# A vision-transformer layer with sliding-window attention: second query halves read 132 keys as a block of 128 and a corner of 4, and patch parts go two to a step

## The chip, the cores and the metric

The kernel runs on one core of one Trainium2 chip. The metric is the device time of one execution in microseconds (us); lower is better. The core has a matrix engine (PE, with its weight loads listed as PEld), a vector engine (DVE), a scalar engine (ACT), a general engine (POOL) and a queue engine for transfers (SP). They run their own instruction streams in order and wait for each other on semaphores.

## The reference, cut to what matters

64 images of 224 x 224 are cut into 196 patches each and projected to 192 features; a class token makes 197 tokens. Then comes one layer: attention by four experts of 12 heads (16 features a head) with a sliding window, a gated output, and a feed-forward step in which each token goes to one of four experts.

```python
mask = (i[:, None] - i[None, :] >= 0) & (i[:, None] - i[None, :] < 64)
for e in range(4):
    q, k, v = (x @ w[e].T split into 12 heads of 16 for w in (wq, wk, wv))
    attn = softmax(where(mask, q @ k.T / 4, -1e30))
    outs.append((attn @ v) @ wo[e].T)
fused = concatenate(outs)
h = h + silu(fused @ w_gate.T) * (fused @ w_up.T)
h = h + expert_ffn(layernorm(h))     # top expert of four, gelu, 192 -> 768 -> 192
```

A query sees itself and the 63 tokens before it. Queries 128 to 196 therefore need keys 65 to 196 (132 keys), and keys 65 to 68 are seen by queries 128 to 131 only.

## The kernel before

The work is in three parts. A set-up splits all weights into a high and a low f16 part (products of f32 accuracy are made of three f16 ones), writes the feed-forward weights to memory and projects the first two images. A loop of 32 turns (`STEPS`) handles two images a turn. After it 36 tiles of 384 sorted tokens go through the feed-forward step.

One turn of the loop first makes 20 projections (queries, keys, and `v` in 8 pieces; `proj`), then the attention, then the gated output. SP stacks queries and keys by transfers (`stack_queries`, `stack_keys`) and copies rows of `v` (L640). The 197 tokens of an image are two halves, `ROWS` = 128 and 69 queries. The attention is cut into 64 units: unit u is (group g of 6 heads, half, three of its heads `HU`, image) by `unit_of`, so that four units of first halves and four of second halves alternate. A first half meets 128 keys, a second half 138 keys from token 59 on (`KW0`, `KWN`). The second half's keys are turned as two blocks of 69, and `v` holds for each image a tile of tokens 0 to 127, one of tokens 128 to 196, and a copy of tokens 59 to 127 (index 1).

The attention is a pipeline written out by hand; in step s

- PE makes `scores(s)` (mask product L684, score products L689) into one of three banks, a part of the next images' patch projection (`patch_at`, `patch_part`, three matmuls at L258; 24 parts in all), then `turn_p(s - 2)` (f32 transposes, L703) into one of three more banks, then `times_v(s - 5)` (matmuls at L240, the helper `product`);
- DVE copies the finished products once in four steps (L898), takes the minima of the scores (they are negated; L905), subtracts the high part of the turned probabilities to have the low part (L911, unit s - 4), and once in four steps takes reciprocals (L920);
- ACT casts the turned probabilities to f16 (L815, unit s - 3) and makes the exponentials of unit s, one instruction a head (L824);
- POOL adds and scales products (L851, L857). Before the units it moves `h_next` into `h_in` (L864, L865), which `h_moved` tells.

`turn_p(u)` waits for `pt_lo` of unit u - 3, since it writes the same bank, and `scores(u)` for the exponentials of unit u - 3. Patch parts wait once for `embedded`, when DVE has read the first half out of bank 7 (L325). From step 41 on the finished outputs are turned (L738), then gated (L747).

Of the kernel before, what the change touches and what calls it, by code (L numbers as in the profile page):

```python
# [26 lines left out]
TOK = 197  # L27
# [6 lines left out]
E = 4  # L34
# [15 lines left out]
KW0 = (0, TOK - 2 * 69)  # L50
KWN = (128, 138)
# [39 lines left out]
def vit_layer(nc, x_t, wp, tok_bias, wqkv, wo, wgu, gate_w, gate_bc, w1, b1, w2, b2, ident, mask_id,  # L91
# [4 lines left out]
    with ExitStack() as ctx:  # L96
# [69 lines left out]
        pt = pt_f[:].rearrange("p (r s n) -> p r s n", r=PR, s=2)  # L166
        gated = pt_f[:, 0:8 * D].bitcast(F32).rearrange("p (t d) -> p t d", t=4)
# [307 lines left out]
        with nc.Block() as block:  # L475
# [20 lines left out]
            def _(dve):  # L496
# [14 lines left out]
                nc.vector.memset(early[:], FAR)  # L511

# [13 lines left out]
        def proj_psum(n):  # L526
            kind, j = proj[n]
            if kind == "v":
                return bank[n % PB][0:ROWS[j // 4], 0:2 * D]
            return bank[n % PB][:, 0:TP]  # L530

        def proj_target(n, part):
            kind, j = proj[n]
            if kind == "v":
                half, img, _, rows = tile_of(j // 2)
                return v[0:rows, img, 2 * half, 24 * (j % 2):24 * (j % 2) + 24, part * HD:part * HD + HD]
            return (kt if kind == "k" else qt)[:, j, part, :]
# [33 lines left out]

        def split_heads(ap):
            return ap.rearrange("p (h k) -> p h k", h=HU)
# [8 lines left out]
        PATCH_STEP, PATCH_GAP, PATCH_LAG = 0, 1, 1  # L582
# [11 lines left out]
        def patch_at(s):  # L594

            n, half = s - PATCH_STEP, 2 * PATCH_PARTS
            if 0 <= n < half:
                return n
            return n - PATCH_GAP if half <= n - PATCH_GAP < 2 * half else None
# [7 lines left out]
        with nc.Fori(0, STEPS, hint_back_edge=True) as i:  # L607
            with nc.Block(no_gpsimd_drain=True) as block:

                @block.sync  # L610
                def _(sp):
# [25 lines left out]
                    for img in range(PAIR):  # L637

                        sp.wait_ge(S["proj_lo"], v_first + 2 * img + 2)
                        sp.dma_start(v[0:69, img, 1], v[KW0[1]:128, img, 0]).then_inc(S["v_dup"], 16)  # L640
# [7 lines left out]
                def _(pe):  # L648

                    for n, (kind, j) in enumerate(proj):  # L650
# [9 lines left out]
                        if kind == "v":  # L660
                            _, _, c0, rows = tile_of(j // 2)
                            w0 = 2 * D * (j % 2)
                            passes = [(zt1[:, zi, c0:c0 + rows], wqkv_s[:, s, 2, blk, w0:w0 + 2 * D])
# [30 lines left out]
                    def turn_p(u):  # L694
                        _, half, _, _ = unit_of(u)
                        rows, kn, nk = ROWS[half], KWN[half], (128, 69)[half]
# [5 lines left out]
                        for b in range(HU * kn // nk):  # L702
                            mm = nc.tensor.transpose(bank[T_BANK + u % TR][0:nk, b * nk:b * nk + rows],  # L703
                                                     p_slot(u)[:, b * nk:b * nk + nk],
# [3 lines left out]
                    def times_v(u):  # L708
                        g, half, hh, img = unit_of(u)
                        w = u // 4  # L710
                        rows, nk = ROWS[half], (128, 69)[half]
# [7 lines left out]
                        for j in range(HU):  # L719
                            head = HG * g + HU * hh + j  # L720
                            passes = []
                            for b in range(1 + half):
                                c = ((1 + half) * j + b) * nk
                                passes += [(pt[0:nk, u % PR, s, c:c + rows], v[0:nk, img, half + b, head, :])
                                           for s in range(2)]
                            mm = product(o_bank(rows)[:, img, HU * hh + j, :], passes)
# [25 lines left out]
                    for s in range(PIPE):  # L752
                        if s < UNITS:
                            scores(s)
                        n = patch_at(s)
                        if n is not None:
# [37 lines left out]
                def _(act):  # L794
# [12 lines left out]
                    for s in range(PIPE):  # L807
                        u = s - LAG_HI
                        if 0 <= u < UNITS:
                            half = unit_of(u)[1]  # L810
                            nk, n = (128, 69)[half], HU * KWN[half]
# [3 lines left out]
                            nc.scalar.copy(pt[0:nk, u % PR, 0, 0:n], bank[T_BANK + u % TR][0:nk, 0:n]  # L815
# [56 lines left out]
                def _(dve):  # L872
# [18 lines left out]
                    for s in range(PIPE):  # L891
# [15 lines left out]
                        if 0 <= u < UNITS:  # L907
                            half = unit_of(u)[1]
                            nk, n = (128, 69)[half], HU * KWN[half]
                            dve.wait_ge(S["pt_hi"], u + 1)  # L910
                            nc.vector.tensor_tensor(pt[0:nk, u % PR, 1, 0:n], bank[T_BANK + u % TR][0:nk, 0:n],  # L911
                                                    pt[0:nk, u % PR, 0, 0:n], ALU.subtract
# [9 lines left out]
                        n = patch_at(s - PATCH_LAG)  # L922
                        if n is not None and (n + 1) % (2 * PATCH_PARTS) == 0:
# [372 lines left out]
```

## Time and profile before

| | us |
|---|---|
| median of 3 runs (4664.97 to 4667.81) | 4666.91 |
| the profiled execution | 4669.48 |
| its span, first to last instruction | 4667.7 |
| PE busy | 4077.5 (87%) |
| DVE busy | 3705.1 (79%) |
| ACT busy | 3196.0 (68%) |
| POOL busy | 1094.3 (23%) |

The span is what the profile shows from the first to the last instruction; the execution's time is 1.8 us longer. Times of one instruction are its duration, from issue to the end of its last write; matmuls overlap, so one that lasts 0.23 us can follow its forerunner by 0.06. A row of the timeline merges like instructions that follow each other: its first number is when the first begins, its second how long the merged stretch is, "x6" how many there are; in brackets stands how long the engine was idle before it and what ended that. `128*69 128x414` is a matmul with 128 rows of contraction and 69 weight columns, and 128 x 414 moving elements.

### The profile page before, as it was taken

The page shows a single profiled execution, that of the slowest core. Times are in us where ns is not written, and L with a number is a line of the kernel's source. Part 1 is how long each engine was busy: PE and PEld are TensorE (multiplying, and loading weights), DVE is VectorE, ACT ScalarE, POOL GpSimd, SP SyncE. Part 2 cuts the span into 40 slices and gives each one's busy share as a digit, 9 for nine tenths or more (in the row PEclk, how much of TensorE's full clock was granted, in tenths as well). Part 3 has the DMA queues.
Part 4 walks back from the last instruction along what each step waited for, and adds up shares of the span by engine and source line. Part 5 has one row for each costly group of instructions (what it writes and reads, how often), then busy time and mean ns, then how long its engine had stood idle before and what let it go on. Part 6 is the DMA issues. An engine that isn't in the chain of part 4 may idle for free. (4 is left out here: it accounts for less than half of the span.)

```text
span 4667.7 us, 129413 instructions
## 1 busy us (share of the span) xinstructions
PE 4077.5 (87%) x47470; PEld 3108.0 (67%) x47470; DVE 3705.1 (79%) x8870; ACT 3196.0 (68%) x9620; POOL 1094.3 (23%) x1496
## 2 busy tenths in 40 slices
PE   4889888888888998888888889888888888985998
PEld 2667666666666766666666667666666666764776
DVE  4888888888888888888888888888888888885665
ACT  2777777777777777777777777777777777772343
POOL 0222222222222222222222222222222222221222
PEclk7999999999999999999999999999999999997999
DMA  5122222111111222211111122222111111224664
GB/s 184 37 51 53 53 53 51 49 49 47 48 30 47 53 53 53 53 49 47 49 49 33 43 51 53 53 53 51 49 48 47 48 31 47 53 53 157 218 220 163
DMA packets 245909, 307.21 MB, mean 66 GB/s; under 512 B 56426, under 2 KB 223892, under 8 KB 235651
## 3 DMA queue, kind: packets, MB, share of 16 engines
q1 hardware_dynamic: 221794, 227.65, 18.7%
q10 hardware_dynamic: 4608, 38.73, 2.6%
q0 software_dynamic: 18912, 32.58, 2.0%
q8 instruction: 412, 6.75, 0.6%
q14 instruction: 183, 1.49, 0.1%
HBM read 127.06 MB, written 43.10 MB: 36 GB/s over the span
## 5 line engine op out<-in xcount | busy, mean ns | idle before, releaser
L824 ACT ACTIVATE p_s<-bank,smin 128x128 f32<-128x128 f32 (+1 forms) x6144 | 1894.6, 406 | 139.3 <-DVE smin L905 121.3
L905 DVE TENSOR_REDUCE smin<-bank 128x3 f32<-128x384 f32 (+1 forms) x2048 | 1157.4, 565 | 192.3 <-PE bank L689 134.0
L703 PE MATMUL bank<-ident_s,p_s 69*69 69x69 f32 (+1 forms) x9216 | 1093.5, 246 | 142.4 <-DVE pt_f L911 113.1
L911 DVE TENSOR_TENSOR pt_f<-bank,pt_f 128x384 f16<-128x384 f32 (+1 forms) x2048 | 1141.3, 560 | 28.5 <-ACT pt_f L815 28.5
L815 ACT CAST pt_f<-bank 128x384 f16<-128x384 f32 (+1 forms) x2048 | 1085.1, 532 | 52.1 <-PE bank L703 52.1
L703 PEld LDWEIGHTS bank<-ident_s,p_s 69*69 69x69 f32 (+1 forms) x9216 | 792.0, 141 | 363.9 <-issue 301.3
L240 PE MATMUL bank<-v_f,pt_f 69*69 69x33 f16 (+1 forms) x18432 | 881.8, 183 | 0.0
L240 PEld LDWEIGHTS bank<-v_f,pt_f 69*69 69x69 f16 (+1 forms) x18432 | 819.0, 110 | 36.9 <-issue 21.2
L684 PE MATMUL bank<-masks_s,mask_id_s 128*128 128x384 f16 (+1 forms) x2048 | 684.0, 334 | 38.9 <-DVE qt_f L876 24.4
L689 PE MATMUL bank<-stacks_f 128*128 128x256 f16 (+3 forms) x4096 | 686.3, 248 | 0.0
L851 POOL TENSOR_TENSOR w_s<-o_raw 128x192 f32<-128x192 f32 (+1 forms) x512 | 307.3, 600 | 1219.9 <-DVE o_raw L898 1219.9
L240 PE MATMUL bank<-zt,wqkv_s 128*128 128x394 f16 x1920 | 412.3, 379 | 170.4 <-PEq L961 164.0
L689 PEld LDWEIGHTS bank<-stacks_f 128*128 128x128 f16 (+1 forms) x4096 | 429.8, 105 | 131.2
L857 POOL TENSOR_TENSOR w_s<-w_s,o_rcp 128x192 f32<-128x192 f32 (+1 forms) x512 | 261.5, 511 | 780.7 <-DVE o_rcp L920 778.2
L240 PEld LDWEIGHTS bank<-zt,wqkv_s 128*128 128x128 f16 x1920 | 206.3, 110 | 357.5 <-issue 264.3
L747 PE MATMUL bank<-wgu_s,qt_f 128*128 128x384 f16 (+1 forms) x2304 | 405.8, 329 | 0.0
L258 PE MATMUL bank<-wp_s,x_s 128*69 128x192 f16 (+1 forms) x2376 | 324.2, 247 | 55.7 <-PEq L398 41.2
L898 DVE COPY o_raw<-bank 128x396 f32<-128x396 f32 (+1 forms) x512 | 287.3, 561 | 34.5 <-PE bank L240 34.5
L747 PEld LDWEIGHTS bank<-wgu_s,qt_f 128*128 128x128 f16 (+1 forms) x2304 | 235.6, 106 | 116.3 <-issue 4.2
L797 ACT ACTIVATE kt_f<-bank 128x394 f16<-128x394 f32 x192 | 95.9, 500 | 302.0 <-PE bank L240 302.0
L833 ACT CAST qt_f<-bank 128x394 f16<-128x394 f32 x192 | 95.8, 499 | 297.1 <-PE bank L738 297.1
L1155 ACT ACTIVATE gel<-bank,b_t 128x384 f32<-128x384 f32 x216 | 125.5, 581 | 229.4 <-PE bank L240 225.3
(116 smaller groups left out, 4449.7 us busy)
## 6 DMA issues: line engine op xcount, KB each, us to landing
stacks_f<-qt_f SPq DMA_DIRECT2D x768, 73.9 KB, 2.1
stacks_f<-kt_f SPq DMA_DIRECT2D x1536, 36.9 KB, 2.1
wx_t<-wx_d SPq DMA_DIRECT2D x36, 1344.0 KB
x_raw<-x_t_dram ACTq DMA_DIRECT2D x32, 1182.0 KB
rec_t<-rec_d SPq DMA_DIRECT2D x36, 678.0 KB, 4.1
v_f<-v_f SPq DMA_DIRECT2D x64, 213.5 KB
rec_d<-fill_s SPq DMA_DIRECT2D x5, 678.0 KB, 4.1
stacks_f<-w_dram SPq DMA_DIRECT2D x2, 1536.0 KB
```

The lines of the kernel that those rows point to most:

```text
L240: mm = nc.tensor.matmul(psum, stat, mov, start=(n == 0), stop=(n == len(passes) - 1))
L258: mm = nc.tensor.matmul(patch_psum(tt), *passes[p], start=(p == 0), stop=(p == len(passes) - 1))
L684: nc.tensor.matmul(ps, mask_id_s[:, 0:rows], masks_s[:, m0:m0 + HU * kn], start=True, stop=False)
L689: mm = nc.tensor.matmul(ps[:, j0 * kn:j1 * kn], qst[:, g % QS, two, q0:q0 + rows], kst[:, g % KS, h0 + j0:h0 + j1, k0:k0 + kn], start=Fals ...
L703: mm = nc.tensor.transpose(bank[T_BANK + u % TR][0:nk, b * nk:b * nk + rows], p_slot(u)[:, b * nk:b * nk + nk], ident_s[0:rows, 0:rows])
L747: mm = nc.tensor.matmul(bank[GU_BANKS[tt]][0:rows, 0:2 * D], ot[:, b, zi, c0:c0 + rows], wgu_s[:, s, b, :], start=(b == 0 and s == zi == 0 ...
L815: nc.scalar.copy(pt[0:nk, u % PR, 0, 0:n], bank[T_BANK + u % TR][0:nk, 0:n]).then_inc(S["pt_hi"], 1)
L824: ins = nc.scalar.activation(p_slot(s)[:, j * kn:j * kn + kn], bank[s % SR][0:rows, j * kn:j * kn + kn], ACT.Exp, scale=-1.0, bias=smin[0: ...
L851: nc.gpsimd.tensor_tensor(mine, o_raw[0:rows, w % 2, :, :, 0:HD], o_raw[0:rows, w % 2, :, :, HD:2 * HD], ALU.add).then_inc(S["o_summed"], 1)
L898: nc.vector.tensor_copy(o_raw[0:rows, w % 2], o_bank(rows)).then_inc(S["o_copied"], 1)
L905: nc.vector.tensor_reduce(least, ps, AX_X, ALU.min).then_inc(S["min_ready"], 1)
L911: nc.vector.tensor_tensor(pt[0:nk, u % PR, 1, 0:n], bank[T_BANK + u % TR][0:nk, 0:n], pt[0:nk, u % PR, 0, 0:n], ALU.subtract).then_inc(S[" ...
```

## The change

Second halves now take 132 keys, from token 65 on. Keys 69 to 196 are a block of 128 that is transposed as one. Keys 65 to 68, seen by the first four queries only, form the corner: an f32 matmul multiplies the probabilities of the first 128 of the 132 keys with the first four columns of the identity and so writes them, for four queries, into four columns beside the block. The turned unit is 3 x 73 = 219 columns over 128 rows, where it was 414 over 69. `times_v` then makes two pairs of products for each head as before, now over 128 rows: the block with a tile of `v` that holds tokens 69 to 196, and 69 columns of which four are the corner and 65 stay zero, with a tile of `v` whose first four rows are tokens 65 to 68 and whose others stay zero. These zeros are written once, in the set-up; the turned probabilities of second halves move to the room of `w1_s`, free once `wx_out` tells that the weights are written. The patch parts go two to a step, in steps 0 to 5 and 8 to 13, where they went one to a step, in 0 to 11 and 13 to 24.

```diff
--- before.py
+++ after.py
@@ -47,8 +47,11 @@
 HM = HID // 128
 ROWS = (128, TOK - 128)
 QW = (0, 128)
-KW0 = (0, TOK - 2 * 69)
-KWN = (128, 138)
+EDGE = 4
+KW0 = (0, TOK - 128 - EDGE)
+KWN = (128, 128 + EDGE)
+PTN = (128, TOK - 128 + EDGE)
+PT2 = 2 * (TOK - 128)
 UNITS = G * 8
 WSCALE = 256.0
 INV = 1.0 / WSCALE
@@ -164,6 +167,8 @@
         smin = sb1("smin", [128, XR, HU])
         pt_f = sb1("pt_f", [128, PR * 2 * HU * KWN[1]], F16)
         pt = pt_f[:].rearrange("p (r s n) -> p r s n", r=PR, s=2)
+        pt_late = w1_s[:].rearrange("p s b e n -> p (s b e n)")[:, 0:PR * 2 * HU * PT2].rearrange(
+            "p (r s n) -> p r s n", r=PR, s=2)
         gated = pt_f[:, 0:8 * D].bitcast(F32).rearrange("p (t d) -> p t d", t=4)
         o_raw = sb1("o_raw", [128, 2, PAIR, HG, VW])
         o_rcp = sb1("o_rcp", [128, 2, PAIR, HG, 1])
@@ -509,6 +514,9 @@
                 nc.vector.memset(zt2[:], 0.0)
                 nc.vector.memset(rec[:], 0.0)
                 nc.vector.memset(early[:], FAR)
+                nc.vector.memset(v[:, :, 1], 0.0)
+                dve.wait_ge(wx_out, 16 * (3 * E + 2))
+                nc.vector.memset(pt_late, 0.0)
 
         nc.all_engine_barrier(sems_to_clear=per_turn)
 
@@ -526,14 +534,14 @@
         def proj_psum(n):
             kind, j = proj[n]
             if kind == "v":
-                return bank[n % PB][0:ROWS[j // 4], 0:2 * D]
+                return bank[n % PB][:, 0:2 * D]
             return bank[n % PB][:, 0:TP]
 
         def proj_target(n, part):
             kind, j = proj[n]
             if kind == "v":
-                half, img, _, rows = tile_of(j // 2)
-                return v[0:rows, img, 2 * half, 24 * (j % 2):24 * (j % 2) + 24, part * HD:part * HD + HD]
+                half, img, _, _ = tile_of(j // 2)
+                return v[:, img, 2 * half, 24 * (j % 2):24 * (j % 2) + 24, part * HD:part * HD + HD]
             return (kt if kind == "k" else qt)[:, j, part, :]
 
         def proj_src(n):
@@ -569,6 +577,16 @@
             c0 = u % XR * HU * KWN[1]
             return p_s[0:ROWS[unit_of(u)[1]], c0:c0 + HU * KWN[unit_of(u)[1]]]
 
+        def probs(u, hl):
+
+            if unit_of(u)[1]:
+                return pt_late[:, u % PR, hl].rearrange("p (h n) -> p h n", h=HU)
+            return pt[:, u % PR, hl, 0:HU * 128].rearrange("p (h n) -> p h n", h=HU)
+
+        def turned_probs(u):
+            n = PTN[unit_of(u)[1]]
+            return bank[T_BANK + u % TR][:, 0:HU * n].rearrange("p (h n) -> p h n", h=HU)
+
         def split_heads(ap):
             return ap.rearrange("p (h k) -> p h k", h=HU)
 
@@ -579,7 +597,7 @@
 
         OT_STEP, OT_GAP, OT_HI, OT_LO = 41, 3, 1, 2
 
-        PATCH_STEP, PATCH_GAP, PATCH_LAG = 0, 1, 1
+        PATCH_STEP, PATCH_GAP, PATCH_LAG, PATCH_RATE = 0, 2, 1, 2
 
         GU_STEPS = {64: 0, 69: 1, 70: 2, 74: 3}
         LN_STEPS = (70, 74)
@@ -593,10 +611,12 @@
 
         def patch_at(s):
 
-            n, half = s - PATCH_STEP, 2 * PATCH_PARTS
+            half = 2 * PATCH_PARTS
+            n = PATCH_RATE * (s - PATCH_STEP)
             if 0 <= n < half:
-                return n
-            return n - PATCH_GAP if half <= n - PATCH_GAP < 2 * half else None
+                return range(n, n + PATCH_RATE)
+            n -= PATCH_RATE * PATCH_GAP
+            return range(n, n + PATCH_RATE) if half <= n < 2 * half else ()
 
         def turned_at(s):
 
@@ -637,7 +657,7 @@
                     for img in range(PAIR):
 
                         sp.wait_ge(S["proj_lo"], v_first + 2 * img + 2)
-                        sp.dma_start(v[0:69, img, 1], v[KW0[1]:128, img, 0]).then_inc(S["v_dup"], 16)
+                        sp.dma_start(v[0:EDGE, img, 1], v[KW0[1]:KW0[1] + EDGE, img, 0]).then_inc(S["v_dup"], 16)
                     stack_keys(1)
                     for g in range(1, G):
                         stack_queries(g)
@@ -658,9 +678,10 @@
                         if n >= PB:
                             pe.wait_ge(S["proj_lo"], n - PB + 1)
                         if kind == "v":
-                            _, _, c0, rows = tile_of(j // 2)
+                            _, _, c0, _ = tile_of(j // 2)
+                            c0 += j // 4 * (TOK - 256)
                             w0 = 2 * D * (j % 2)
-                            passes = [(zt1[:, zi, c0:c0 + rows], wqkv_s[:, s, 2, blk, w0:w0 + 2 * D])
+                            passes = [(zt1[:, zi, c0:c0 + 128], wqkv_s[:, s, 2, blk, w0:w0 + 2 * D])
                                       for s, blk, zi in D_PASSES]
                         else:
                             m = 0 if kind == "q" else 1
@@ -693,22 +714,28 @@
 
                     def turn_p(u):
                         _, half, _, _ = unit_of(u)
-                        rows, kn, nk = ROWS[half], KWN[half], (128, 69)[half]
+                        rows, kn = ROWS[half], KWN[half]
+                        turned = bank[T_BANK + u % TR]
                         pe.wait_ge(S["p_ready"], u + 1)
                         if u >= TR:
                             pe.wait_ge(S["pt_lo"], u - TR + 1)
                         else:
                             pe.wait_ge(S["proj_lo"], last_use(T_BANK + u))
-                        for b in range(HU * kn // nk):
-                            mm = nc.tensor.transpose(bank[T_BANK + u % TR][0:nk, b * nk:b * nk + rows],
-                                                     p_slot(u)[:, b * nk:b * nk + nk],
+                        for j in range(HU):
+                            c0, k0 = j * PTN[half], j * kn
+                            if half:
+                                nc.tensor.matmul(turned[:, c0 + rows:c0 + rows + EDGE],
+                                                 p_slot(u)[:, k0:k0 + 128], ident_s[0:rows, 0:EDGE],
+                                                 start=True, stop=True)
+                                k0 += EDGE
+                            mm = nc.tensor.transpose(turned[:, c0:c0 + rows], p_slot(u)[:, k0:k0 + 128],
                                                      ident_s[0:rows, 0:rows])
                         mm.then_inc(S["pt_mm"], 1)
 
                     def times_v(u):
                         g, half, hh, img = unit_of(u)
                         w = u // 4
-                        rows, nk = ROWS[half], (128, 69)[half]
+                        rows = ROWS[half]
                         pe.wait_ge(S["pt_lo"], u + 1)
                         if u == 0:
                             pe.wait_ge(S["lg_read"], 1)
@@ -718,12 +745,10 @@
                             pe.wait_ge(S["o_copied"], w)
                         for j in range(HU):
                             head = HG * g + HU * hh + j
-                            passes = []
-                            for b in range(1 + half):
-                                c = ((1 + half) * j + b) * nk
-                                passes += [(pt[0:nk, u % PR, s, c:c + rows], v[0:nk, img, half + b, head, :])
-                                           for s in range(2)]
-                            mm = product(o_bank(rows)[:, img, HU * hh + j, :], passes)
+                            o = o_bank(rows)[:, img, HU * hh + j, :]
+                            passes = [(probs(u, hl)[:, j, rows * b:rows * b + rows], v[:, img, 2 * half - b, head, :])
+                                      for b in range(1 + half) for hl in range(2)]
+                            mm = product(o, passes)
                         mm.then_inc(S["pv_mm"], 1)
 
                     def turn_o(e, blk):
@@ -752,8 +777,7 @@
                     for s in range(PIPE):
                         if s < UNITS:
                             scores(s)
-                        n = patch_at(s)
-                        if n is not None:
+                        for n in patch_at(s):
                             if n == 0:
                                 pe.wait_ge(S["x_lo"], 1)
                                 pe.wait_ge(S["pos_read"], 1)
@@ -808,11 +832,10 @@
                         u = s - LAG_HI
                         if 0 <= u < UNITS:
                             half = unit_of(u)[1]
-                            nk, n = (128, 69)[half], HU * KWN[half]
                             act.wait_ge(S["pt_mm"], u + 1)
                             if u >= PR:
                                 act.wait_ge(S["pv_mm"], u - PR + 1)
-                            nc.scalar.copy(pt[0:nk, u % PR, 0, 0:n], bank[T_BANK + u % TR][0:nk, 0:n]
+                            nc.scalar.copy(probs(u, 0)[:, :, 0:PTN[half]], turned_probs(u)
                                            ).then_inc(S["pt_hi"], 1)
                         if s < UNITS:
                             half = unit_of(s)[1]
@@ -906,10 +929,9 @@
                         u = s - LAG_LO
                         if 0 <= u < UNITS:
                             half = unit_of(u)[1]
-                            nk, n = (128, 69)[half], HU * KWN[half]
                             dve.wait_ge(S["pt_hi"], u + 1)
-                            nc.vector.tensor_tensor(pt[0:nk, u % PR, 1, 0:n], bank[T_BANK + u % TR][0:nk, 0:n],
-                                                    pt[0:nk, u % PR, 0, 0:n], ALU.subtract
+                            nc.vector.tensor_tensor(probs(u, 1)[:, :, 0:PTN[half]], turned_probs(u),
+                                                    probs(u, 0)[:, :, 0:PTN[half]], ALU.subtract
                                                     ).then_inc(S["pt_lo"], 1)
                         w = window_at(s, LAG_OR)
                         if w is not None:
@@ -919,8 +941,8 @@
                                 dve.wait_ge(S["o_ready"], w - 1)
                             nc.vector.reciprocal(o_rcp[0:rows, w % 2], o_raw[0:rows, w % 2, :, :, 2 * HD:VW]
                                                  ).then_inc(S["o_rcp_ready"], 1)
-                        n = patch_at(s - PATCH_LAG)
-                        if n is not None and (n + 1) % (2 * PATCH_PARTS) == 0:
+                        done = [n for n in patch_at(s - PATCH_LAG) if (n + 1) % (2 * PATCH_PARTS) == 0]
+                        for n in done:
                             half = n // (2 * PATCH_PARTS)
                             if half == 0:
                                 dve.wait_ge(S["h_moved"], 1)
```

## Rows read from the trace of the kernel before

**Rows 1.** The page: busy us of each engine, share of the span, instructions.

```profile
PE 4077.5 (87%) x47470; PEld 3108.0 (67%) x47470; DVE 3705.1 (79%) x8870; ACT 3196.0 (68%) x9620; POOL 1094.3 (23%) x1496
```

**Rows 2.** Table by stretches: length, busy us by engine (instructions), granted clock, DMA share, GB/s.

```profile
1016.81:1096.82 80.01, 75.01 (x1074) 62.38 (x1074) 73.92 (x164) 75.67 (x254) 19.89 (x32) 1.00 0.24 61
```

**Rows 3.** Timeline of PE in one turn: start us, length us, engine, line, operation, operands.

```profile
1016.81 0.32 PE L684 MATMUL bank<-masks_s,mask_id_s 128*128 128x384 f16 x1 [0.45 <-DVE kt_f L876]
...
1018.31 0.34 PE L684 MATMUL bank<-masks_s,mask_id_s 128*128 128x384 f16 x1 [0.76 <-DVE qt_f L876]
...
1018.65 0.41 PE L258 MATMUL bank<-wp_s,x_s 128*128 128x192 f16 x3
1018.90 0.33 PE L684 MATMUL bank<-masks_s,mask_id_s 128*128 128x384 f16 x1
...
1036.15 0.32 PE L684 MATMUL bank<-masks_s,mask_id_s 128*128 128x384 f16 x1
...
1051.24 0.56 PE L240 MATMUL bank<-v_f,pt_f 69*69 69x33 f16 x12
1051.65 0.34 PE L684 MATMUL bank<-masks_s,mask_id_s 128*69 128x414 f16 x1
...
1052.01 0.49 PE L703 MATMUL bank<-ident_s,p_s 128*128 128x128 f32 x3
1052.34 0.57 PE L240 MATMUL bank<-v_f,pt_f 69*69 69x33 f16 x12
...
1055.40 0.34 PE L684 MATMUL bank<-masks_s,mask_id_s 128*69 128x414 f16 x1
...
1056.36 0.32 PE L684 MATMUL bank<-masks_s,mask_id_s 128*128 128x384 f16 x1
...
1057.15 0.56 PE L703 MATMUL bank<-ident_s,p_s 69*69 69x69 f32 x6 [0.30 <-DVE pt_f L911]
1057.56 0.31 PE L240 MATMUL bank<-v_f,pt_f 128*128 128x33 f16 x6
1057.71 0.32 PE L684 MATMUL bank<-masks_s,mask_id_s 128*128 128x384 f16 x1
...
1066.23 0.32 PE L684 MATMUL bank<-masks_s,mask_id_s 128*128 128x384 f16 x1
...
1097.61 0.56 PE L703 MATMUL bank<-ident_s,p_s 69*69 69x69 f32 x6 [0.64 <-DVE pt_f L911]
```

**Rows 4.** Timeline of DVE in the same turn, steps 31 and 32.

```profile
1055.96 0.58 DVE L905 TENSOR_REDUCE smin<-bank 69x3 f32<-69x414 f32 x1 [0.16 <-PE bank L689]
1056.46 0.54 DVE L911 TENSOR_TENSOR pt_f<-bank,pt_f 128x384 f16<-128x384 f32 x1
```

**Rows 5.** Line L470, f32 products: durations min/median/max; whole run, its start, and timeline.

```profile
L470 PEld LDWEIGHTS bank<-kt_f,qt_f x32: 190/190/337, 14.6 to 27.0; 96*128 96x128 f32 x32
L470 PE MATMUL bank<-kt_f,qt_f x32: 486/486/1007, 14.6 to 27.3; 96*128 96x384 f32 x32
...
L470 PEld LDWEIGHTS bank<-kt_f,qt_f x2: 286/310/333, 14.6 to 14.8; 96*128 96x128 f32 x2
...
L470 PE MATMUL bank<-kt_f,qt_f x2: 847/927/1007, 14.6 to 15.4; 96*128 96x384 f32 x2
...
14.62 0.50 PEld L470 LDWEIGHTS bank<-kt_f,qt_f 96*128 96x128 f32 x2 [14.62 <-DMA kt_f<-wgu_dram]
```

**Rows 6.** Groups by line and shape: busy us, mean ns of one, idle us before them.

```profile
L911 DVE TENSOR_TENSOR pt_f<-bank,pt_f 69x414 f16<-69x414 f32 x1024 | 586.6, 575 | 28.5 <-ACT pt_f L815 28.5
L911 DVE TENSOR_TENSOR pt_f<-bank,pt_f 128x384 f16<-128x384 f32 x1024 | 557.3, 544 | 0.0
L703 PEld LDWEIGHTS bank<-ident_s,p_s 69*69 69x69 f32 x6144 | 467.3, 142 | 223.8 <-issue 189.1
```

**Rows 7.** Timeline of POOL in the same turn.

```profile
1008.89 0.50 POOL L865 COPY h_in<-h_next 69x384 f32<-69x384 f32 x1
```

**Rows 8.** The set-up: timeline of DVE, and table by stretches as in rows 2.

```profile
85.25 1.19 DVE L509 MEMSET zt<- 128x1359 f16 x1 [0.35 <-issue]
...
78.00:84.00 6.00, 2.59 (x16) 1.43 (x13) 4.11 (x15) 0.80 (x2) 0.77 (x1) 0.77 0.00 0
```

## The prediction

> **What bounds the kernel now.** I read the page first, then the loop's turns by stretches, then single steps. The page puts PE at 87% of the span, DVE at 79% and ACT at 68% [rows 1]: near each other, so it names no bound. The table by stretches shows that of one turn 80.0 us pass while its 64 units are scored, and in them PE, DVE and ACT all look over nine tenths full [rows 2]. With 32 turns this stage is 2560 us, over half the time. Busy times of matmuls overlap, so I read it from start to start.
>
> PE, at the upper clock level (granted clock 1.00 [rows 2]): scores of a first half take 0.34 us (1018.31 to 1018.65), of a second half 0.36 (1051.65 to 1052.01); a patch part 0.25 (1018.65 to 1018.90); `turn_p` of a first half 0.33 (1052.01 to 1052.34), of a second 0.41 (1057.15 to 1057.56), which falls to 0.39 where its first load is hidden; `times_v` 0.15 (1057.56 to 1057.71) and 0.41 (1051.24 to 1051.65) [rows 3]. Eight units come to 4 x 0.82 + 4 x 1.16 = 7.9 us. But step 32 begins at 1056.36 and step 40 at 1066.23: 9.87 us [rows 3]. PE alone is not the bound.
>
> What closes the step is a loop over two steps, and the rows show it whole. The scores of step 31 begin at 1055.40 [rows 3], the minima at 1055.96, the subtraction behind them at 1056.46, lasting 0.54 [rows 4]; only then may `turn_p` write its bank again, at 1057.15, "0.30 <-DVE"; `times_v` follows at 1057.56 and the scores of step 33 at 1057.71 [rows 3]. That is 2.31 us for two steps: 1.75 up to the turning, then 0.41 + 0.15. With the other combinations of halves (turning 0.33, `times_v` 0.41, a slower subtraction) the eight loops are about 2.31 three times, 2.6, 2.51 three times, 2.24, sum 19.3; each step lies in two, so eight steps take 9.65 us. DVE's two copies of `o_raw` ahead of minima add some 0.2. This meets the observed 9.87, so I price the change with this loop.
>
> **The change part by part.** *Corner products.* The six transposes of a second half (0.39 us, 0.06 each) become, for each of three heads, an f32 product with 128 weight columns and 4 moving ones, and a transpose with 128 weight columns and 69 moving ones, which I leave at 0.06. For the product the nearest rows are the 16 of L470. They are 32 records, two for each product, each with a weight load [rows 5]. With 384 moving columns the load is hidden there; with four it lies bare. Its price, first way: the first load starts at 14.62 and takes 0.286; the two loads together end 0.50 after 14.62, so 0.21 after the first. The matmul lasts 0.847 or more there and 0.486 later [rows 5], so this is the lower level, and at the upper one 0.21 is 0.105. Second way, at the upper level: a product's load lasts 0.190 [rows 5], a transposing load 0.142 [rows 6] with 0.06 from one to the next: 0.190 - 0.142 + 0.06 = 0.11. I take 0.11 a record: 3 x (2 x 0.11 + 0.06) = 0.84 us for the turning, +0.45 for each of the 32 second halves of a turn. From below I bound a record by a transposing load, 0.06 (turning 0.54); from above by 0.19, loads that overlap nothing (1.32). The value taken comes twice from rows of the same form, so it is far nearer than either end.
>
> A rule speaks against the change here. The Trainium skill, "TensorE: Matmul & The Clock Gate", section "LDWEIGHTS (loading the stationary operand)", says that a weight load costs its columns, whatever the depth of the contraction: P / 1.2 ns, 107 ns for 128 columns; few moving columns don't help. The Trainium skill, "FP8 and Floating Point Precision", section "TensorE Precision Notes", has four passes for true f32. The rows agree with the 107 ns and show two records, not four loads; by four, the turning would be an estimated 1.5 us, near my upper end.
>
> *Narrower second halves.* 396 score columns instead of 414 save 0.01 on PE and 0.02 in the minima. The subtraction runs over 219 columns instead of 414. Its two forms, 414 and 384 columns, last 0.575 and 0.544 [rows 6], 0.001 a column, so it gets 0.20 shorter; nothing, if the new strided operand eats it. ACT's cast shrinks in the same way, but ACT is not in the loop above. What pays is the 0.20 inside the loop, in four of eight steps.
>
> *`times_v` of second halves.* Twelve matmuls before and after, now over 128 rows of the contraction with 69 weight columns. The form is not shown; the two that are cost 0.41 / 12 = 0.034 and 0.15 / 6 = 0.025 a matmul [rows 3]. I leave 0.034; the other end would give back 0.1 a unit.
>
> *The new loop.* By turned unit (second halves first) the loops are 1.75 + 0.84 + 0.15 = 2.75 three times, 2.82, 2.30 three times, 2.23. PE's own work is 1.35, 1.35, 1.33, 1.58 in the steps that turn second halves and 1.07, 1.07, 1.09, 0.84 in the others, 9.7 us. Where the loop asks more than PE's own work the step is longer: 1.61, 1.35, 1.40, 1.58, 1.07, 1.23, 1.09, 1.14, and 0.15 for a copy, 10.6 us against 9.87, +0.75. Steps 16 to 63 are six such groups: +4.5 us.
>
> *Patch parts two a step.* The same 24 parts of 0.24, now in steps 0 to 5 and 8 to 13. Spread out they lay in gaps of the loop; step 9 will hold 0.33 + 0.48 + 0.84 + 0.41 = 2.06 us of PE alone, with `turn_p`, and so ACT's cast, queued behind the parts. Step 1 cannot start before 1018.31, 1.5 us after step 0 at 1016.81 [rows 3], since its bank waits for projections. From there PE needs 0.81, 1.14, 1.14, 1.16, 1.32, 1.35, 1.35 to step 8 and 1.81, 2.06, 1.55, 1.55, 1.57, 1.32, 1.35, 1.35 to step 16: 22.3 us with the 1.5. Before, step 16 began at 1036.15, after 19.3 [rows 3]: +3.0 us. The gap of two steps hides PE's wait for `embedded`. DVE's wait for `h_moved` moves up to step 6, with the minima queued behind it; POOL's second copy starts at 1008.89, long before [rows 7]: nothing.
>
> *Drain.* The turnings of units 62 and 63 come behind the last scores, the first at 1097.61 after waiting 0.64 for DVE [rows 3]: 2 x 0.45 less 0.2 of subtraction, +0.7.
>
> *Copies and projections of v.* The copy on SP's queue carries 4 rows instead of 69 and is due only in step 9; the second tiles' products get 128 weight columns instead of 69 under the same 384 moving ones: nothing.
>
> *Set-up.* DVE fills 3168 and 3312 more f16 at the end of a block. 1359 f16 took 1.19 us [rows 8], 0.88 ns each: 5.7 us, or half where two are filled as one word; +4 once. The new wait for `wx_out`, with these fills and the block's barrier behind it, costs nothing: the DMA share is already 0.00 from 78 to 84 us, before DVE gets there [rows 8].
>
> Sum: 3.0 + 4.5 + 0.7 = 8.2 us a turn; x 32 = 262; + 4 = 266. The profiled execution took 4669.5 us (span 4667.7): 4935.5. The median of the runs, 4666.9, lies 2.6 lower: **4933 us, 5.7% slower**. This case's own range: with no loop waits at all in steps 16 to 63 (+0 there) 32 x 3.7 + 4, 4790; with two microseconds more waiting a turn, 5000.
>
> **The rivals.** *Cheap products, faster* (the other side). If a four-column record costs what a transposing load costs, 0.06, the turning is 0.54 and the loops 2.45 three times, 2.5, 2.30 three times, 2.23: 19.0 against 19.3, and DVE has more room for its copies; some -0.4 us in eight steps, -2.4 over six groups, +0.7 in the crowded patch steps, +0.1 in the drain: -1.6 x 32 + 4, 4620 us. It decides below some 0.07 a record. For it: DVE and ACT do look full, and the change relieves both. Against: both ways of pricing the load.
>
> *Nothing moves.* At 0.07 to 0.08 a record gain and price meet, 4667.
>
> *Bare records.* At 0.19 a record PE alone needs 4 x 0.82 + 4 x 2.08 = 11.6 us in eight steps: +10.4 over six groups, +5.9 before step 16, +1.7 in the drain, 18 us a turn, 5240. For it: the switch between product and transpose is seen nowhere. Against: the first two loads of L470 follow each other without a gap [rows 5]. The four-pass rule, if it held in loads, would end near it.
>
> **How the numbers follow.** Forecast case 0.77, cheap products 0.12, nothing 0.04, bare records 0.07. A measurement here can tell about 0.2%, 9 us, from no change. Slower 0.84, same 0.04, faster 0.12. Leaving out the cheap case and most of the bare one, and leaning a little past the own range for record prices from 0.10 to 0.12, the range is 4730 to 5030.
>
> **What would show it.** Right: two records of an f32 product for each head, 0.11 apart; `turn_p` of a second half over 0.8 us; the subtraction of 219 columns 0.20 shorter and DVE idle before minima, waiting for PE; steps 32 to 40 in 10.6 us; step 9 over 2 us. Wrong: a turning under 0.55 us, or DVE still full.

## The result, and the profile after

The changed kernel takes 5491 us at the median of 4 runs (5486 to 5495), against 4667 for the kernel before on the same chip: ratio 1.1765, 95% interval 1.1745 to 1.1786. It is 17.6% slower; 5.7% was forecast, and the time lies 461 us above the range. The profiled execution has a span of 5488.4 us.

Here is the page after, with the same line as [rows 1] and the granted clock in 40 slices, in tenths (before, all but two of them were 9):

```profile
PE 4930.5 (90%) x50542; PEld 4004.3 (73%) x50542; DVE 3545.2 (65%) x8872; ACT 3133.8 (57%) x9620; POOL 1091.3 (20%) x1496
...
PEclk7888888888888888888888888888888888887999
```

DVE and ACT are relieved and stand at 65% and 57% of a longer span; PE has 3072 more matmuls. And the clock, which the forecast never asked about, is below nine tenths through the whole loop: mean 0.856 where it was 0.957.

The table by stretches of one turn shows where. The first line is steps 0 to 15 with all patch parts, the others follow up to step 43 (columns as in [rows 2]):

```profile
1198.76:1221.39 22.63, 22.11 (x289) 20.52 (x290) 16.87 (x42) 17.04 (x60) 6.64 (x8) 1.00 0.40 119
1221.39:1233.40 12.01, 11.60 (x162) 10.07 (x158) 9.50 (x23) 10.21 (x37) 2.22 (x4) 1.00 0.22 46
1233.40:1240.20 6.80, 6.80 (x61) 6.17 (x61) 3.23 (x9) 3.56 (x13) 1.11 (x2) 0.50 0.27 58
1240.20:1247.00 6.80, 6.40 (x88) 5.44 (x86) 5.29 (x13) 5.84 (x20) 1.10 (x2) 1.00 0.05 11
1247.00:1253.80 6.80, 6.80 (x59) 6.18 (x58) 3.13 (x9) 3.60 (x12) 1.11 (x2) 0.50 0.27 58
1253.80:1260.70 6.90, 6.50 (x89) 5.52 (x87) 5.47 (x13) 5.88 (x20) 1.11 (x2) 0.99 0.06 13
1260.70:1267.50 6.80, 6.80 (x59) 6.20 (x60) 2.82 (x8) 3.20 (x12) 0.91 (x2) 0.50 0.26 57
```

In this trace the clock holds the upper level while patch parts run (1.00), and 12 us more; from then on it changes between 0.50 and 1.00, and in the stretch shown it does so every 6.8 us. At 0.50 PE gets through 59 to 61 matmuls where it gets through 88 or 89 at 1.00, and it has no idle time in them. Summed from 110 us on, the lower level lasts 1518 us (337 before). On the mean of the 32 turns 33 us of it lie in the 101 us from the first scores to the last, all in steps 16 to 63; before there was none there, and its 337 us all lay outside (9.0 us a turn between the last scores and the next first ones). So the kernel before changed level too, but never within the stretch whose steps the forecast read.

The timeline of PE gives the price of the turning at each level. At the upper one (compare 1057.15 in [rows 3]):

```profile
1243.63 0.35 PE L727 MATMUL bank<-ident_s,p_s 69*128 69x4 f32 x2 [0.28 <-DVE pt_f L933]
1243.84 0.26 PE L731 MATMUL bank<-ident_s,p_s 69*128 69x69 f32 x1
1243.93 0.33 PE L727 MATMUL bank<-ident_s,p_s 69*128 69x4 f32 x2
...
1244.41 0.26 PE L731 MATMUL bank<-ident_s,p_s 69*128 69x69 f32 x1
1244.51 0.31 PE L245 MATMUL bank<-v_f,pt_f 128*128 128x33 f16 x6
1244.66 0.34 PE L705 MATMUL bank<-masks_s,mask_id_s 128*69 128x396 f16 x1
```

1243.63 to 1244.51 is 0.88 us, 0.29 a head, in two records for each product; 0.84 was forecast. At the lower level a like turning takes from 1248.28 to 1249.88, 1.60 us:

```profile
1248.28 0.53 PE L727 MATMUL bank<-ident_s,p_s 69*128 69x4 f32 x2
...
1249.88 0.89 PE L245 MATMUL bank<-v_f,w_s 128*69 128x33 f16 x12
```

Who waits for it is named in the waits of the kernel after (total us, times, longest); in the kernel before the first of these was 134.0, the second 121.3:

```profile
DVE smin L928 <- PE bank L710: 883.9, 1156, 2.8
ACT p_s L847 <- DVE smin L928: 863.1, 1414, 2.3
```

### The profile page after: what moved, and what is told of

Its sections match the earlier page's. It is cut to its first block and busy times, and to the rows that moved or that the text cites. A ratio compares the mean times of both kernels' runs of the same rounds, so it can differ in the third digit from the quotient of the medians.

```text
span 5488.4 us, 135559 instructions
## 1 busy us (share of the span) xinstructions
PE 4930.5 (90%) x50542; PEld 4004.3 (73%) x50542; DVE 3545.2 (65%) x8872; ACT 3133.8 (57%) x9620; POOL 1091.3 (20%) x1496
## 5 line engine op out<-in xcount | busy, mean ns | idle before, releaser
L731 PE MATMUL bank<-ident_s,p_s 128*128 128x128 f32 (+1 forms) x6144 | 1457.6, 295 | 16.1
L731 PEld LDWEIGHTS bank<-ident_s,p_s 128*128 128x128 f32 (+1 forms) x6144 | 1199.7, 209 | 60.3 <-issue 54.0
L727 PEld LDWEIGHTS bank<-ident_s,p_s 69*128 69x128 f32 x6144 | 1040.5, 229 | 145.6 <-issue 114.1
L727 PE MATMUL bank<-ident_s,p_s 69*128 69x4 f32 x6144 | 1051.2, 254 | 63.9 <-DVE pt_f L933 63.5
L245 PEld LDWEIGHTS bank<-v_f,w_s 128*69 128x69 f16 x12288 | 707.0, 137 | 7.3
L245 PE MATMUL bank<-v_f,w_s 128*69 128x33 f16 x12288 | 681.5, 199 | 0.0
L933 DVE TENSOR_TENSOR pt_f<-bank,pt_f 128x384 f16<-128x384 f32 x1024 | 556.8, 544 | 0.0
L838 ACT CAST pt_f<-bank 128x384 f16<-128x384 f32 x1024 | 496.4, 485 | 0.0
L838 ACT CAST w_s<-bank 128x219 f16<-128x219 f32 x1024 | 359.5, 351 | 152.5 <-PE bank L731 132.9
L933 DVE TENSOR_TENSOR w_s<-bank,w_s 128x219 f16<-128x219 f32 x1024 | 383.9, 378 | 88.8 <-ACT w_s L838 88.8
```

What stands on the lines that cost most here:

```text
L245: mm = nc.tensor.matmul(psum, stat, mov, start=(n == 0), stop=(n == len(passes) - 1))
L727: nc.tensor.matmul(turned[:, c0 + rows:c0 + rows + EDGE], p_slot(u)[:, k0:k0 + 128], ident_s[0:rows, 0:EDGE], start=True, stop=True)
L731: mm = nc.tensor.transpose(turned[:, c0:c0 + rows], p_slot(u)[:, k0:k0 + 128], ident_s[0:rows, 0:rows])
L838: nc.scalar.copy(probs(u, 0)[:, :, 0:PTN[half]], turned_probs(u)).then_inc(S["pt_hi"], 1)
L933: nc.vector.tensor_tensor(probs(u, 1)[:, :, 0:PTN[half]], turned_probs(u), probs(u, 0)[:, :, 0:PTN[half]], ALU.subtract).then_inc(S["pt_lo ...
```

## The experiments

Theory A: the corner products do it twice over. Their bare weight loads (loads that no moving columns cover) cost what the forecast said, and while they load, few columns move, and the clock falls. Theory B: the clock was held up by patch parts spread over 25 steps, and drawing them together let it fall. The runs came in three groups, each on a chip of its own, on which the kernel before took 4742, 4737 and 4710 us; so I compare ratios to the kernel before on the same chip: e1 to e4 are on the first of these, e5 to e8 on the second, e9 to e12 on the third. Clocks are those of each run's profiled execution.

| run | ratio, 95% interval | mean clock |
|---|---|---|
| the change | 1.1765 (1.1745 to 1.1786) | 0.856 |
| e1 before, two parts a step | 1.0074 (1.0047 to 1.0101) | 0.955 |
| e2 change, one part a step | 1.1761 (1.1698 to 1.1823) | 0.864 |
| e3 change, no corner | 0.9711 (0.9685 to 0.9737) | 0.957 |
| e4 change, 64 moving columns | 1.0948 (1.0916 to 1.0980) | 0.933 |
| e5 change, small transposes | 1.1650 (1.1594 to 1.1707) | 0.850 |
| e6 as e5, one part a step | 1.1563 (1.1538 to 1.1589) | 0.861 |
| e7 before, products added | 1.2355 (1.2316 to 1.2394) | 0.835 |
| e8 change, 32 moving columns | 1.1077 (1.1048 to 1.1107) | 0.920 |
| e9 change, full transposes | 0.9957 (0.9940 to 0.9973) | 0.958 |
| e10 as e9, one part a step | 0.9779 (0.9764 to 0.9793) | 0.967 |
| e11 the change again | 1.1866 (1.1823 to 1.1910) | 0.850 |
| e12 before again, one run | 4711.5 us | 0.966 |

**Which half of the change.** e1 gives the kernel before the new `patch_at`:

```diff
-        PATCH_STEP, PATCH_GAP, PATCH_LAG = 0, 1, 1
+        PATCH_STEP, PATCH_GAP, PATCH_LAG, PATCH_RATE = 0, 2, 1, 2
```

> The kernel before with the patch parts two to a step (steps 0 to 5 and 8 to 13) and nothing else of the change. Theory A (the corner products take the clock down: they keep PE occupied with weight loads while four columns move): the mean granted clock stays near 0.95 and only the crowded steps cost, 1 to 2 us a turn, so 4700 to 4730 us. Theory B (the patch parts spread over 25 steps had held the clock up, and drawing them into 14 steps lets it fall): the clock falls in steps 14 to 63, mean below 0.90, time 4900 us or more.

e2 takes it from the changed kernel:

```diff
-        PATCH_STEP, PATCH_GAP, PATCH_LAG, PATCH_RATE = 0, 2, 1, 2
+        PATCH_STEP, PATCH_GAP, PATCH_LAG, PATCH_RATE = 0, 1, 1, 1
```

> The changed kernel with its patch parts one to a step again (steps 0 to 11 and 13 to 24). Theory A: steps 0 to 24 hold the upper level as before, but steps 25 to 63 still fall, so 5300 to 5480 us, mean clock 0.86 to 0.89. Theory B: the clock is back near 0.95 and the time is that of the blind sum, 4900 to 4950 us.

The clock of e1 stays at 0.955 and that of e2 stays down at 0.864. Theory B falls as the cause of the loss. Patch parts do hold the clock where they run and shortly after: in steps 16 to 31 e2, with parts up to step 24, has no lower level at all and the change 11.0 us a turn, but from step 32 on e2 has 22.8 us (mean of 32 turns). Two parts a step cost 0.7% on the kernel before; e1 took 4778 us, more than the 4730 I gave, but on a chip where the kernel before takes 75 more. e2's 5565 lies above its 5480 for the same reason; its ratio is as that of the change.

**The corner.** e3 deletes the product, so keys 65 to 68 are left out for queries 128 to 131:

```diff
-                                nc.tensor.matmul(turned[:, c0 + rows:c0 + rows + EDGE],
-                                                 p_slot(u)[:, k0:k0 + 128], ident_s[0:rows, 0:EDGE],
-                                                 start=True, stop=True)
```

> The changed kernel without the three corner products of a second half; keys 65 to 68 are left out for queries 128 to 131. Theory A: clock back near 0.95, the turning of a second half about 0.2 us (three transposes), DVE and ACT relieved, so 4500 to 4620 us, below the kernel before. Theory B: the patch parts are still drawn together, so the clock still falls and the time is 4900 us or more. A third view, that the strided operands or the zero columns cost much, would show as more than 4750 us at a clock of 0.95.

Ratio 0.971 at a clock of 0.957, 4605 us, as Theory A wanted: three transposes in place of six, narrower scores, 219 columns and products over 128 rows together gain 2.9%, in spite of two parts a step. All of the loss is in the corner. e7 is the counterpart, the kernel before with nothing but the products:

```diff
+                        for j in range(HU * half):
+                            nc.tensor.matmul(bank[T_BANK + u % TR][:, 420 + 4 * j:424 + 4 * j],
+                                             p_slot(u)[:, j * kn:j * kn + 128], ident_s[0:rows, 0:4],
+                                             start=True, stop=True)
```

> The kernel before with the three f32 products of 128 weight columns and 4 moving columns added to each second half, their result going to unused columns of the bank; nothing else changed. Theory A: the products alone make both the price and the fall of the clock. At the upper level 0.6 us a second half, some 500 us in all; with the clock below 0.90 some 500 us more: 5500 to 5900 us, ratio 1.18 to 1.26. If the clock fell for another reason (operands over 128 rows, the narrower scores), it stays at 0.95 and the ratio is 1.09 to 1.13.

1.2355 and 0.835. Its PE timeline also has the six records alone, without transposes between them: 0.64 us, 0.107 a record, at the upper level.

```profile
1344.45 0.78 PE L703 MATMUL bank<-ident_s,p_s 69*128 69x4 f32 x6
1345.09 0.57 PE L707 MATMUL bank<-ident_s,p_s 69*69 69x69 f32 x6
```

**Load or clock.** e4 and e8 keep every instruction and every weight load, and only move more columns (e8 has 32 in both places):

```diff
-                                nc.tensor.matmul(turned[:, c0 + rows:c0 + rows + EDGE],
-                                                 p_slot(u)[:, k0:k0 + 128], ident_s[0:rows, 0:EDGE],
+                                nc.tensor.matmul(turned[:, c0 + rows:c0 + rows + 64],
+                                                 p_slot(u)[:, k0:k0 + 128], ident_s[0:rows, 0:64],
```

> The changed kernel with one size changed: each corner product moves 64 columns of the identity, not 4; the 60 extra ones are written over by the transposes behind. The same two records and the same weight loads, more work. Theory A, with the moving columns as what holds the clock: the clock rises to 0.93 or more and the time falls to 4900 to 5050 us although more is computed. If the clock looked at how long PE is occupied, or if the loads alone were the cost, the time stays at 5490 us or rises by up to 100 us.

> The changed kernel with 32 moving columns in each corner product, between the 4 of the change (ratio 1.177, clock 0.856) and the 64 of e4_wide_corner (1.095, 0.933). If the moving columns hold the clock, both lie between: ratio 1.12 to 1.16, clock 0.88 to 0.92. If 64 columns worked through another way (a longer matmul hiding a load), the clock stays at 0.856 and the ratio at 1.17 or above.

More work, less time: from 1.18 with 4 columns to 1.108 with 32 and 1.095 with 64, the clock going from 0.856 to 0.920 and 0.933. Their ends were a little off (e4 took 5185 us, not 5050 or less; e8's ratio is below 1.12). The turning of e4 costs at the upper level what that of the change costs, 0.29 us a head, so the columns bought nothing but clock.

Where they bought it shows in steps 16 to 63 of one turn, first of e4, then of the change (columns as in [rows 2]):

```profile
1160.21:1224.61 64.40, 62.08 (x865) 54.41 (x861) 52.05 (x122) 55.31 (x193) 12.79 (x23) 1.00 0.15 34
1221.39:1299.19 77.80, 75.46 (x865) 66.42 (x861) 52.36 (x122) 56.61 (x193) 12.78 (x23) 0.80 0.13 28
```

The same 865 matmuls, at 1.00 and at 0.80. In none of its 32 turns has e4 any lower level in these steps; e8 has 4.1 us a turn there, the change 32.8 (31.5 in e11, on another chip). What e4 has left of it, 8.2 us a turn, lies in steps 0 to 15. On its chip the kernel before with two parts a step (e1) has 2.5 us there too, and the change on the third chip (e11) 6.8, so that part depends on the chip as well.

Timeline of PE in e4, a head's records and the start of the next head's, and then the start of steps 32 and 40:

```profile
1206.03 0.38 PE L727 MATMUL bank<-ident_s,p_s 69*128 69x64 f32 x2
1206.25 0.23 PE L731 MATMUL bank<-ident_s,p_s 69*128 69x69 f32 x1
1206.32 0.38 PE L727 MATMUL bank<-ident_s,p_s 69*128 69x64 f32 x2
```

```profile
1181.88 0.32 PE L705 MATMUL bank<-masks_s,mask_id_s 128*128 128x384 f16 x1
...
1192.71 0.32 PE L705 MATMUL bank<-masks_s,mask_id_s 128*128 128x384 f16 x1
```

Between the last two lie 10.83 us, with the clock up. In the trace of the change itself, 29 of the 160 groups of eight steps between step 16 and 56 hold no lower level at all: they average 10.80 us, and steps 32 to 40 take 10.83 like those of e4. The 114 that hold more than 6 us of it average 14.46, with 7.9 us at the lower level. Of these 32 are steps 40 to 47, which with the clock up take 11.64 (e4); place by place the 114 would average 11.04 with the clock up. So (14.46 - 11.04) / 7.9 = 0.43 us are lost for each microsecond of the lower level.

**A smaller corner.** If bare loads of 128 columns cost so much, load four:

```diff
+                                nc.tensor.transpose(turned[0:EDGE, c0 + rows:c0 + rows + EDGE],
+                                                    p_slot(u)[0:EDGE, k0:k0 + EDGE], ident_s[0:EDGE, 0:EDGE])
```

> The changed kernel with the corner turned by a transpose of 4 rows and 4 columns (a weight load of 4 columns, 4 moving columns) in place of the f32 product with 128 weight columns; the rows 4 to 127 of those columns keep what the bank held and meet zero rows of v. Theory A: clock at 0.95 as without a corner, three more short matmuls of 0.03 to 0.06 us a second half, so a ratio of 0.97 to 0.985 to the kernel before. If a mode switch or an f32 matmul with few moving columns as such were at fault, the ratio stays above 1.05.

> As e5_small_corner, with the patch parts one to a step again. Drawing them together cost 0.7% on the kernel before, so this should be the fastest of all, ratio 0.955 to 0.975. If the two parts a step pay once DVE and ACT are relieved, it is slower than e5_small_corner.

Both were wrong by far: 1.165 and 1.156, clock 0.85 and 0.86, with no f32 product left. The timeline of e5 at the upper level says why the price stays:

```profile
1759.99 0.08 PEld L727 LDWEIGHTS bank<-ident_s,p_s 4*4 4x4 f32 x1
1759.99 0.16 PE L727 MATMUL bank<-ident_s,p_s 4*4 4x4 f32 x1
1760.08 0.14 PEld L730 LDWEIGHTS bank<-ident_s,p_s 69*128 69x128 f32 x1
1760.09 0.28 PE L730 MATMUL bank<-ident_s,p_s 69*128 69x69 f32 x1
...
1760.29 0.08 PEld L727 LDWEIGHTS bank<-ident_s,p_s 4*4 4x4 f32 x1
```

The small load begins 0.21 us after the full transpose in front of it started, where in e9 below one full transpose follows another after 0.06. A head takes 0.30 us, as with the product. So my wording of Theory A was too narrow: what the change, e5, e6 and e7 share is not the f32 product, but turnings of 0.9 us or more in which PE hardly moves columns, be it for bare loads or for small weights that wait. Why the small load starts so late is open.

**Full transposes.** e9 turns the corner's 128 keys for all 69 queries and lets the next head write over what is too much:

```diff
-                                nc.tensor.matmul(turned[:, c0 + rows:c0 + rows + EDGE],
-                                                 p_slot(u)[:, k0:k0 + 128], ident_s[0:rows, 0:EDGE],
-                                                 start=True, stop=True)
+                                nc.tensor.transpose(turned[:, c0 + rows:c0 + rows + rows],
+                                                    p_slot(u)[:, k0:k0 + 128], ident_s[0:rows, 0:rows])
```

> The changed kernel with each corner turned by a transpose of the same 128 keys for all 69 queries (128 weight columns, 69 moving ones) in place of the f32 product; the 65 columns too many are written over by the next head's, or lie behind the last. It has six transposes as the kernel before, 0.06 us apart, so a turning of 0.39 us, and no small weight tile. If the two losses are the bare loads and the clock, both go: clock 0.95 or more, ratio 0.975 to 0.995. If a corner as such costs (reading the probabilities twice, 128 weight columns), the ratio stays above 1.03.

> As e9_full_turn, with the patch parts one to a step again: 0.5 to 1% faster than e9_full_turn, ratio 0.965 to 0.99, below the kernel before. If two parts a step pay once DVE and ACT are relieved, it is slower than e9_full_turn.

Timeline of PE in e9; the turning lasts from 1205.53 to 1205.93, 0.40 us, as in [rows 3]:

```profile
1205.53 0.25 PE L727 MATMUL bank<-ident_s,p_s 69*128 69x69 f32 x1 [0.28 <-DVE pt_f L932]
1205.62 0.23 PE L730 MATMUL bank<-ident_s,p_s 69*128 69x69 f32 x1
1205.68 0.23 PE L727 MATMUL bank<-ident_s,p_s 69*128 69x69 f32 x1
...
1205.93 0.31 PE L245 MATMUL bank<-v_f,pt_f 128*128 128x33 f16 x6
```

Both losses are gone: 0.9957, just above the band, clock 0.958. With one part a step e10 takes 4605 us, ratio 0.978: 2.2% less than the kernel before, and 17.7% less than the change on the same chip (e11, 5593 us). Two parts a step cost 1.9% here (4692 against 4605), more than the 0.5 to 1% expected: steps 0 to 15 take 22.9 us in e9 and 20.7 in e10 (means of 32 turns).

**The same kernels on another chip.**

> The changed kernel itself, on the chip of the other experiments, for its ratio there: 1.17 to 1.18 as on the first chip, clock 0.86; so that e2_after_one_part, e4_wide_corner and e8_corner_32 are compared on one chip.

> The kernel before on this chip, for its profile: 4740 us where the first chip took 4667. If the 70 us are slower stacking transfers, the first eight steps of a turn wait on them and take more than the 7.9 us seen on the first chip, and steps 32 to 40 stay at 9.87.

The two ran on the chip of e9 and e10, not on those of e2, e4 and e8 as e11's expectation had it, and e12 took 4711 us, not 4740. e11 has 1.187, just above its band: the change's ratio differs by some 1% between two chips, so e2's gain over the change, if there is one, is not settled below that. In e12 steps 0 to 7 take 10.9 us on the mean of the turns instead of 8.8, nearly all of the 2.1 in steps 5 and 6 (4.5 against 2.5), and steps 32 to 40 still 9.87. The stretch between the last scores and the next turn's first gives back 0.9, which leaves 42 us in the span. The place is shown. That stacking transfers cause it is not: in both traces they land 2.1 us after their issue at the median and 3.0 to 3.1 at nine tenths of them.

## Why the prediction was right or wrong

*The way:* right. Slower, and bare loads of f32 products are one of two causes; the larger one, the clock, the forecast did not have.

*The price of a record:* right, at the upper level. 0.105 and 0.11 were read from [rows 5, 6]; in e7 six records take 0.64 us, 0.107 each, and from load to load its products take 0.111 at the upper level and 0.213 at the lower one (medians). The rule on weight loads (the Trainium skill, "TensorE: Matmul & The Clock Gate", "LDWEIGHTS (loading the stationary operand)"), 107 ns for 128 columns, agrees at the upper level and not at the lower one. Of the four passes (the Trainium skill, "FP8 and Floating Point Precision", "TensorE Precision Notes") only two records with two loads are seen. In moving columns four would fit: at the upper level a record of L470 with 384 f32 columns takes 0.32 us to the next one, where the mask product with 384 f16 columns (L684) takes 0.16.

*The subtraction:* right. 0.378 for 219 columns against 0.575 [rows 6], 0.20 shorter, strided operands or not; the cast 0.351 against 0.552:

```profile
L838 ACT CAST w_s<-bank 128x219 f16<-128x219 f32 x1024 | 359.5, 351 | 152.5 <-PE bank L731 132.9
L933 DVE TENSOR_TENSOR w_s<-bank,w_s 128x219 f16<-128x219 f32 x1024 | 383.9, 378 | 88.8 <-ACT w_s L838 88.8
```

*The loop over two steps:* right, at the level at which it was read. 10.6 us forecast for steps 32 to 40, 10.83 measured where the clock is up; e4, whose steps 16 to 63 take 64.4 us, against 59.7 before, has +4.7 where +4.5 was forecast.

*The crowded patch steps:* right. Steps 0 to 15 take 22.63 us (forecast 22.3, before 19.3), step 9 takes 2.07 (forecast 2.06). `times_v` kept its 0.41 over 128 rows.

*The drain and the projections:* wrong. From the last scores to the next turn's first it takes 53.5 us, not 49.9: +3.6, of which 0.7 was forecast. Projections were said not to change; between the last scores and the next first ones the lower level lasts 13.2 us a turn, 9.0 before.

*Set-up:* the two fills take 1.38 and 1.44 us, and the first turn's projections start at 91.9 instead of 89.5: +2.4, forecast +4.

*What failed:* one premise, written down at the start, "PE, at the upper clock level", and carried over to a kernel in which PE's work is of another kind. Every term is a duration at 1.00, the sum is a time at 1.00, and none of the rivals has the clock in it. Per turn the excess is 18.7 us in steps 16 to 63, 3.3 in steps 0 to 15 and 3.6 outside. Of these, 4.7 (e4) + 3.3 + 0.7 (the drain's, forecast and not measured apart) = 8.7 is what the forecast priced at 8.2. In steps 16 to 63 the other 14.0 are the clock: 78.4 us against the 64.4 of e4, with the same number of records and no lower level (e4 ran on another chip, but the kernel before takes 59.7 us in these steps both in its first trace and in e12). Outside, 2.9 are left; the 4.2 us more at the lower level make 1.8 of them at 0.43, and 1.1 stays open. Times 32: 278 us of price, 506 us of clock and 35 us open, together 819 of the 821 by which the span grew. The other way from the sum of the lower level gives the same: (1518 - 337) x 0.43 = 508.

*The sign of the warning* was in the sum itself. The forecast replaced, in half of the units, 0.39 us of closely packed matmuls by 0.84 us of which 0.66 load weights. It took that as PE being busier, and never asked what PE would be doing. Nor did it use that the kernel before already ran 9 us a turn at the lower level, between the scored stretches.

## What to carry to other kernels

Here an f32 product with 4 moving columns cost its two weight loads, 0.107 us each: take such a price from the nearest f32 product's loads, not from its small operand. When a change puts long stretches of loads, or of small weights that wait, into PE's work (here four turnings of 0.88 us in 10.8), forecast it at both clock levels, since here, in steps 16 to 63, the clock took three times what the loads took (14.0 against 4.7 us a turn). To turn a corner, a full transpose whose surplus is written over cost 0.06 us here and beat both the product and the small transpose.

## What the runs showed of the hardware that was not expected

The clock fell to 0.50 in stretches of 6.8 us although PE had no idle time in them and hardly any around them (6.40 and 6.50 us busy of 6.8 and 6.9); before it fell PE had done turnings of 0.88 us with 4 moving columns in 6 of 9 matmuls. With 32 or 64 moving columns in the same 0.29 us a head it was at the lower level for 4.1 us or not at all in steps 16 to 63 of a turn, against 32.8; with steps 0 to 15 it was 10.0 and 8.2. With six full transposes in 0.40 us, and PE idle more (4.1 us of steps 16 to 63 in e9, 2.3 in e4, 2.2 in the change), it fell for 1.6 us in steps 0 to 15 (e9) or not at all (e10). So idle time does not tell these kernels apart. What exactly sets the granted clock these runs don't show.

A transpose of 4 x 4 among transposes with 128 weight columns takes 0.30 us a pair in e5, where two full ones take 0.13 in e9; the load of 4 columns lasts 0.08 but begins 0.21 us after the load of the full transpose in front of it.

Chips differ in the first steps of a turn: 8.8 us on one, 10.9 on another for steps 0 to 7 of the same kernel, with a span 42 us longer in all.
